# The written-out order of five in-order engines, made anew for a sampling, scan and mixture-of-experts kernel

## The reference, cut to what matters

```python
q_feat = bilinear_sample(feature_map, ref)                # 1024 points
off = gelu(layer_norm(q_feat @ W_o1 + b_o1)) @ W_o2 + b_o2
sampled = bilinear_sample(feature_map, ref + off * scale) # 1024 x 8 points
keys, values = sampled @ W_k.T, sampled @ W_v.T
attn = softmax(q . k / sqrt(8)); out = sum(attn * values) # [1024, 64]
h = concat([out, txt])                                    # [1152, 64]
h = h + recurrence(_layernorm(h))
h1, h2 = x @ w1[e], x @ w2[e]                             # x = _layernorm(h), 16 experts
h = h + sum_e(dispatch[e] * ((silu(h1) * h2) @ w3[e]))    # dispatch: top 2 of 16
```

## Time and profile before

| | us |
|---|---|
| timed runs, median (lowest, highest) | 2320.62 (2315.28, 2321.72) |
| profiled execution, whole time | 2306.16 |
| span of its instructions | 2304.3 |
| PE busy | 2034.4 (88%) |
| DVE busy | 1995.7 (87%) |
| POOL busy | 1690.9 (73%) |
| ACT busy | 941.8 (41%) |
| mean granted TensorE clock | 0.949 of full |

### The profile page before, as it was taken

How to read it: one execution, slowest core, us unless ns; L and a number is a source line. 1 busy time by engine, 2 the same in 40 slices (tenths; PEclk the granted TensorE clock), 3 DMA queues, 4 the chain that set the end, 5 groups by cost and what they waited for, 6 DMA issues and landing times.

```text
span 2304.3 us, 46464 instructions
## 1 busy us (share of the span) xinstructions
PE 2034.4 (88%) x15249; PEld 1842.3 (80%) x15249; DVE 1995.7 (87%) x6209; ACT 941.8 (41%) x2040; POOL 1690.9 (73%) x2169
## 2 busy tenths in 40 slices
...
GB/s 204 219 198 174 180 78 186 158 181 182 141 167 111 174 174 167 183 162 173 112 169 153 169 182 168 177 91 192 135 171 182 169 178 110 178 110 71 69 16 6
DMA packets 363149, 346.84 MB, mean 151 GB/s; under 512 B 49312, under 2 KB 313632, under 8 KB 362784
## 3 DMA queue, kind: packets, MB, share of 16 engines
...
## 4 chain that ended last, share of the span: by engine, by line
PE 40%; DVE 27%; POOL 17%; issue 11%; DMA 4%; ACT 1%; DVEq 0%; SPq 0%; POOLq 0%
POOL gath L574 11%; PE bank_o L637 10%; PE bank_h L628 6%; PE bank_d L693 6%; PE bank_h L629 6%; PE bank_d L703 5%; DVE ob L975 5%; POOL rest L581 4%; DVE wsam L1053 4%; DMA gath<-table,idx 4%; DVE hid L964 3%; DVE v_sb L1088 2%; DVE v_sb L1081 2%; PE bank_a L715 1%; DVE k_sb L1059 1%
## 5 line engine op out<-in xcount | busy, mean ns | idle before, releaser
L574 POOL DMA_INDIRECT gath<-table,idx x1024 | 1137.7, 1111 | 268.4 <-issue 238.9
L637 PEld LDWEIGHTS bank_o<-w_sb,hid 128*128 128x128 f32 x4608 | 629.8, 197 | 68.7 <-issue 60.7
L637 PE MATMUL bank_o<-w_sb,hid 128*128 128x64 f32 x4608 | 626.4, 274 | 30.4 <-DVE ob L975 29.9
L628 PE MATMUL bank_h<-xsplit,w 128*128 128x384 f32 x1536 | 611.8, 398 | 37.7 <-DVE hid L964 35.5
L787 ACT ACTIVATE silu<-bank_h 128x384 f32<-128x384 f32 x768 | 380.3, 495 | 439.2 <-PE bank_h L629 431.5
L629 PE MATMUL bank_h<-xsplit,w 128*128 128x384 f32 x1536 | 530.3, 345 | 0.0
L975 DVE SCALAR_TENSOR_TENSOR ob<-bank_o,disp,ob 128x64 f32<-128x64 f32 x2160 | 475.4, 275 | 4.8 <-PE bank_o L637 4.4
L581 POOL MEMSET rest<- 1x400 f32 x1024 | 432.3, 422 | 29.6
L964 DVE TENSOR_TENSOR hid<-silu,bank_h 128x384 f32<-128x384 f32 x768 | 420.0, 547 | 25.7 <-ACT silu L787 20.5
L693 PE MATMUL bank_d<-eye,wsam 128*128 128x128 f32 x2048 | 295.1, 291 | 83.8 <-DVE wsam L1053 82.4
L1053 DVE TENSOR_TENSOR wsam<-gath,cw 128x1024 f32<-128x1024 f32 x256 | 311.8, 1218 | 60.6 <-DMA gath<-table,idx 52.1
...
## 6 DMA issues: line engine op xcount, KB each, us to landing
...
xin<-x_dram SPq DMA_DIRECT2D x256, 256.0 KB
...
gath<-table,idx POOLq DMA_INDIRECT x1024
...
```

Of the source, the lines that this page charges most:

```text
L574: pool.indirect_dma_start(out=gath[buf][:, p, :, :].rearrange("p a c -> p (a c)"), out_offset=None, in_=table[par], in_offset=bass.Indirec ...
L628: mm(bank[:, 0:GC], w12[:, e, which, 0, :], xsplit[gp][:], start=True, stop=False)
L637: last = mm(bank_o[n % 2][:, C * k:C * (k + 1)], hid[:, n % HB, 128 * k:128 * (k + 1)], w3_sb[:, e, :], start=True, stop=True)
```

## The change

Every string of ORDER is written anew. The pieces, their number, their code, their waits and the buffers are the same; each engine has the same multiset of pieces (PE 2752, DVE 2768, ACT 1712, POOL 624, SP 256). The new strings were made from the durations that the last profile shows. Start of the POOL strings and of the DVE strings:

```diff
 ORDER = {
...
     "dve": (
-        "efhjkkmmnkkmmnkkmmnkkmmeknfBhkCjmDmknrkstmkmunvxkwyGmzGkmGnHGHGHGHkGHGHGHGHmGkmHnGBHGHHCkDGrmkmsntGHGHHukvHmxkmwnyGzrkGGsHtGHemGkm
...
+        "efhjkkmmnkkmmnkkmmnkekfhmjkmnBkCDmmrnkstkuvmxmnkwyGzHGkGGHGHmGHkmGnHGHGHGHkGHGHGHmGHkmGnHBGHHCkDHrmkmnsteukvfmhxmnkwjyGzkrGGHmsGtH
...
     "pool": (
-        "eoooooooooooooooooooeoooooorooovooooooooooorooovooorooeoovooooooooroooovoooooooooorooovoooorooooovoo",
+        "eoooooooooooooooooeoooooorooovooooooooooooorooeovooooroooovooooooorooooovooooooooorooovoooorooooovoo",
...
 }
```

More of the change, by code:

```diff
@@ new lines @@
+        "tFGuFlGFmGFmwGFlGFyGFGFGFalGFmGamFGFlGFsGFtGFGlFumGFmGFbblGFbbGbFbwbFGbcldmeGmFylGFGFGFGlFGmFmGFlGFs",
+        "GtFGFGulFhGmiFmGFGlFaaaGalFwmGFmGFyGFlGaFGaFaaGFGaFGFGFlsGFtmGFmGFulGFGlFaGFmGFmwGFlGFyGlFGmFGmFaGFl",
+        "GFalaGFmGFsmGtFaGlFaGFuFGalGFmbbGmFbbGbFbbwbGFclGFyGlFGmFGmFdGFlGFeGlFmGFsmGtFGlFGFuGFlhGFimGFmaaGFw",
+        "aGFaGFyFGaaGFaGaFGFGFlGFGFlsGFtmGFmGFulGFGlFaGFmGFmwGFlGFyGlFGmFaGmFaGFlGFaGlFamGFsmGtFaGlFaGFuFGalG",
+        "FmbbGmFbbGbFbwbGbFclGFyGlFGmFGmFdGFlGFeGFlmGFsmGtFGlFGFuhGiFGFlGmFamaGFwaGFaGFyFGaaGFaGaFGFGFlGFGFls",
@@ new lines @@
+        "GFtmGFmGFulGFGlFaGFmGFmwGFlGFyGlFGmFaGmFaGFlGFaGlFamGFsmGtFaGlFaGFuFGalGFmbbGmFbbGbFbwbGbFclGFyGlFGm",
+        "FGmFdGFlGFeGFlmGFsmGtFGlFGFuGhFiGlFGmFamaaGFwaGFGFyaFGaaGFaGFGFGFlGFGFlsGFtmGFmGFulGFGlFaGFmGFmwGFlG",
+        "FyGlFGmFaGmFaGFlGFaGlFamGFsmGtFaGlFaGFuFGalGFmbbGmFbbGbFbwbGbFclGFyGlFGmFGmFdGFlGFeGFGlmFsmGtFGFlGFu",
+        "GhFiGFGlmFamaGFwaGFaGFyFGaaGFaGaFGFGFlGFGFlsGFtmGFmGFulGFGlFaGFmGFmwGFlGFyGlFGmFaGmFaGFlGFaGlFamGFsm",
+        "GtFaGlFaGFuFGalGFmbbGmFbbGbFbwbGbFclGFyGlFGmFGmFdGFlGFeGFGlmFsmGtFGFlGFuhGiFGFlGmFamaaGFwGaFGFyaFGaa",
@@ new lines @@
+        "GFaGFGFGFlGFGFlsGFtmGFmGFulGFGlFaGFmGFmwGFlGFyGlFGmFaGmFaGFlGFaGlFamGFsmGtFaGlFaGFuFGalGFmbbGmFbbGbF",
+        "bwbGbFclGFyGlFGmFGmFdGFlGFeGFlmGFsmGtFGlFGFuGhFiGlFGmFamaaGFwaGFaGFyFGaaGFaGFGFGFlGFGFlsGFtmGFmGFulG",
+        "FGlFaGFmGFmwGFlGFyGlFGmFaGmFaGFlGFaGlFamGFsmGtFaGlFaGFuFGalGFmbbGmFbbGbFbwbbGFclGFyGlFGmFGmFdGFlGFeG",
+        "FlmGFsmGtFGlFGFuGhFiGFlmGFmaaGFwGaFaGFyFGaaGFaGaFGFGFlGFGFlsGFtmGFmGFulGFGlFaGFmGFmwGFlGFyGlFGmFaGmF",
+        "aGFlGFaGlFamGFsmGtFaGlFFauGalGFmGFbmbbbbbGFGFwbGbFclGFyGlFGmFGmFdGFlGFeGFlmGFsmGtFGlFGFuhGiFGlFGmFam",
@@ new lines @@
+        "aaGFwGaFGFyaFGaaGFaGFGFGFlGFGFlsGFtmGFmGFulGFGlFaGFmGFmwGFlGFylGFGmFaGmFaGFlGFaGFlaGmFsmGtFaGlFaGFuF",
+        "GalGFmbbGmFbbGbFbwbbGFclGFyGlFGmFGmFdGFlGFeGFlmGFsmGtFGFlGFuGhFiGFlGmFamaaGFwaGFGFyaFGaaGFaGFGFGFlGF",
+        "GFlsGFtmGFmGFulGFGlFaGFmGFmwGFlGFyGlFGmFaGmFaGFlGFaGFlaGmFsmGtFaGlFaGFuFaGbblGFmGbmFbGbFbbbwGcFdlGFy",
+        "lGFGmFGmFGFlGeFGFlGFmsGmtFGlFGFuhGiFGlFGmFamaGFwaGFaGFyFGaaGFaGaFGFGFlGFGFlsGFtmGFmGFulGFGlFaGFmGFmw",
+        "GFlGFyGlFGmFaGmFaGFlGFaGFlaGmFsmGtFaGlFaGFuFGalGFmbbGmFbbGbFbbwbGFclGFyGlFGmFGmFdGFlGFeGFGlmFsmGtFGF",
@@ new lines @@
+        "sGtmGmGGGlaGmGmwGGGlyGmGmaGGalaGmGsmGtaGBaGGalGmGmGwbGcGGlyGmGmdGGGlmGsmGtGgGGlhGmGmaaGwaGBGaGaaGyaG",
+        "aGGGGlsGtmGmGGGlaGmGmwGGGlyGmaGmaGGaGlamGsmGtaGBaGGalGmGmGwGbcGGlyGmGmdGGGlmGsmGtGgGhGGlGmamaGwaGBGa",
+        "GaaGyaGaGGGGlsGtmGmGGGlaGmGmwGGGlyGmaGmaGGaGlamGsmGtaGBaGGalGmGmGwGbcGGlyGmGmdGGGlmGsmGtGgGGhGlGmama",
+        "aGwaGBGaGaaGyaGGGGGlsGtmGmGGGlaGmGmwGGGlyGmaGmaGGaGlamGsmGtaGBaGGalGmGmGwGbcGGlyGmGmdGGGGlmsmGtgGGGh",
+        "GGlmamaGwaGBGaGaaGyaGaGGGGlsGtmGmGGGlaGmGmwGGGlyGmaGmaGGaGlamGsmGtaGBaGGalGmGmGwGbcGGlyGmGmdGGGGlmsm",
```

131 lines of the change are left out of this document (53 added, 78 removed).

## The result

The new lists are slower: median 2339.85 us of eight runs (2332.67 to 2349.94), before 2314.46 of eight on the same chip; ratio 1.0112, 95% interval 1.0084 to 1.014. The profiled execution took 2340.5 us, its span 2338.7, 34.4 more than before's. The forecast had the wrong sign.

The account below looks back on a forecast made before the run. A loop of POOL's gathers and DVE's products and indices was taken to bound it. Regular part -5 and start-up -5 us gave -10, 2296 us profiled, 2311 us median; own range 2304 to 2318, whole range 2290 to 2334.

Parts of the forecast that it names:

- The start-up, POOL: Power of batch 1's B1 moves two gather pieces earlier on POOL; lag made up later, 0, other bound +4.5 us.
- The start-up, DVE: Around 250 us, batch 2's B1 and B2 fill DVE's waits for a gather and keys: -5 us, bounds 0 and -18.
- P1(b; 0) on POOL: This power stands one gather piece sooner on POOL: 0, or +1.0 us a period if later D1(b; 7, 1) gives no cover.
- D1(b; 7, 1): DVE's product of the last half group moves later, so its gather wait goes: -1.0 us a period, bounds 0 and -1.26.
- D1(b; 4, 0): DVE's product in the middle moves ahead of one X, its gather wait growing by that: +0.55 us a period.
- D3(b; 3, 0): Moves one X and one Z earlier on DVE; its 0.94 us wait passes to D1(b; 4, 0): value 0.
- PE behind D2: PE stands while ACT copies samT where D3 directly follows D2: costed 0, without cover +1.4 us a period.
- Gathers stretch: Rival, chance 0.08: new neighbours lengthen POOL's gathers, 1.0 us a period, +16 us over sixteen batches less 5; 2331 us.
- POOL takes over: Rival, chance 0.16: POOL's start-up lag stays and the earlier P1(b; 0) waits each period, +15 us less 2; 2334 us.

Follow-up runs that it names:

- The kernel with the last half group: Old lists with only D1, D2 and D3 of the last point group placed as in the new lists, batches 4 to 14; 2308.93 us, ratio 0.9984.

## Why the prediction was wrong

How far one execution can be trusted: four with the old regular lists have periods of 133.0 to 133.6 us (mean 133.4), four with the new ones 134.7 to 135.7 (mean 135.1). With the old start, seven have their fifth index write at 605.3 to 614.8 us (mean 609.8; the profile before has the lowest); with the new, five at 617.8 to 624.5 (mean 621.8). So by the profiles the new start costs about 12 us and the new periods 1.7 x 11 = 19. Together that is 31, while the timed medians differ by 25: such sums are good to some microseconds. The profile before had the start-up with the earliest fifth index write of the seven, so 6 of its 17.8 us to the new lists are luck.

- *The start-up, POOL: valued 0, "time it can make up".* This step failed, and it is the dearest one that a run shows alone. The wait of 10 us was foreseen (11.7), but the variance did not come 2.5 us sooner (159.8 against 160.1 us), P1(0; 0) waited 4.7 besides, and most of the lag stayed to the end. The powers alone cost 12 us on the old lists. POOL's later waits were no spare time; I read this as POOL waiting for a DVE that is itself late by POOL's gathers.
- *The start-up, DVE: -5.* Not found. Without POOL's steps the new start was still at 620 us; D3(1; 1, 0) and (1; 1, 1) wait 1.9 and 1.8 us even so, and 5.8 us are lost later, between the first gathers of batches 2 and 4. A lower granted clock goes with it (0.79 around 270 us); what starts that, and the share of the clock in the loss, is open: no kernel tests it.
- *P1(b; 0) on POOL: value 0, cost 1.0 if the cover goes.* Failed. Alone the step costs 0.5 to 0.7 us a period: the gathers behind it are those of D1(b; 7, 1), which is then late in all eleven batches. In the new lists D1(b; 7, 1) stands later and is late in five, and putting the step back there gained nothing. The wait is 2.4 us in the mean, not 1.0: counted from the last gather that D1(b; 4, 0) needs, POOL reaches the power 4.1 us sooner than before and not 3.6, the variance comes 0.9 us later and not 0.55, and POOL had been 2.7 us late in the mean, not the row's 3.2.
- *D1(b; 7, 1): -1.0.* Right in mechanism, about -0.5 when done alone (by the periods; the timed runs still allow none), and eaten by the former in the new lists.
- *D1(b; 4, 0): +0.55.* The wait grew as foreseen, but the stretch from D1 to P1's variance by 0.78 us: the X, and a wait of D3(b; 4, 0), 0.36 us a period, that was not foreseen.
- *D3(b; 3, 0).* Right: 0.70 to 0.27 us, taken over by D1(b; 4, 0).
- *PE behind D2: 0.* PE now waits for ACT's samT 0.61 us a period at D3(b; 6, 0), which follows its D2 directly in ten of eleven batches, and 0.12 at D3(b; 7, 0), which does so in two and not in many; before, at neither. The kernel with the last half group has the 0.12 and still lost its wait; the 0.61 is in no kernel alone, so what it costs the loop stays open.
- *"Gathers stretch".* True of one instruction, 0.5 us a period, but others are shorter: on the way to D1(b; 4, 0) 0.26, a quarter of what the rival priced.
- *Missing altogether:* the table writes, which make D1(b; 4, 0)'s gathers land up to 3.7 us later than D1(b; 7, 1)'s. I read that wait as POOL's alone. As they land alike in both profiles, this did not turn the forecast's sign.
- *Readings of the rows.* I put nearly all of POOL's 8.9 us of waits for variances at P5(b; 0). It is 5.3; another 2.6 lie at powers between the first gather and D1(b; 4, 0)'s, inside the stretch that POOL paces. And between the intervals of 148 and 150 us and the fifth index write lies one more, of 134.

By segments of the loop the new profile adds up: from the first gather to the end of the last one that D1(b; 4, 0) needs +0.64 (waits of POOL's inner powers 0.33, gather durations 0.26), landing +0.08, from D1(b; 4, 0) to P1's variance +0.78, to P5's variance -0.28, to the index write +0.17, in all +1.39 us a period. This says where the time went, not which move sent it there: of the regular part's steps run alone, none cost more than 0.7 us a period, and taking two of them out of the new lists gave nothing back. That the regular lists cost 1.4 to 1.7 us a period is shown; by which moves is shown only in part. The rival "POOL takes over" (2334) named the right two places and came nearest, but its deciding point was wrong: P5(b; 0) still waits 4.7 us in the mean.
